# Attention output of a three-stage kernel: the block result turned and normalised by other engines, and carried to token layout by 64-byte transfers

## What is computed

```
xn   = layernorm(x)
attn = gamma * concat_heads(softmax(leaky(q k^T / sqrt(2), 0.2)) v) + xn     # 8 heads, q and k of 2, v of 16 channels
ffn  = mixture of experts on rmsnorm(xn): top 2 of 16, 12 of them MLPs 128-512-128, capacity 1024
out  = x + attn + ffn
```

## Time and profile before

| | us |
|---|---|
| median of three runs | 977.33 |
| profiled execution, its own time | 976.61 |
| span of that execution in the trace | 974.8 |
| VectorE busy | 744.3 (76%) |
| TensorE matmul busy | 883.5 (91%) |
| ScalarE busy | 716.5 (74%) |
| GpSimd busy | 581.7 (60%) |

### The profile page before, as it was taken

One profiled execution on the slowest core, in us unless ns is written; L12 is line 12 of the kernel. 1 busy time (PEld: TensorE's weight loads), 2 busy tenths in 40 slices (PEclk: granted clock), 3 DMA queues, 4 the chain that ended last, 5 costly groups with the idle time before them and its releaser, 6 DMA issues.

```text
span 974.8 us, 19803 instructions
## 1 busy us (share of the span) xinstructions
PE 883.5 (91%) x7619; PEld 365.8 (38%) x7620; DVE 744.3 (76%) x851; ACT 716.5 (74%) x859; POOL 581.7 (60%) x574
## 2 busy tenths in 40 slices
PE   0688249999999999999999989999999999999997
PEld 0444102333333333867767723333333333333332
DVE  6698889999999995001011089999999999999996
ACT  0689878888888887454454468888888888888886
POOL 3355137776676662999999015647566574665770
PEclk9999659999999999999999989999999999999999
DMA  8723100101100011242342210010011002002100
GB/s 228 269 65 72 31 27 30 44 30 36 39 25 28 18 52 58 68 135 92 110 135 78 80 43 26 22 49 20 26 32 39 23 21 64 24 13 62 31 7 22
DMA packets 48163, 55.34 MB, mean 57 GB/s; under 512 B 10714, under 2 KB 35122, under 8 KB 48080
## 3 DMA queue, kind: packets, MB, share of 16 engines
q1 hardware_dynamic: 38464, 44.10, 14.8%
q0 software_dynamic: 8192, 9.37, 3.3%
q10 hardware_dynamic: 1424, 0.76, 0.3%
HBM read 31.58 MB, written 30.02 MB: 63 GB/s over the span
## 4 chain that ended last, share of the span: by engine, by line
PE 77%; ACT 9%; DVE 6%; issue 4%; DMA 1%; SPq 1%; POOLq 0%; ACTq 0%; DVEq 0%
PE ps L765 26%; PE ps L745 15%; PE ps L735 13%; PE ps L825 8%; PE ps L817 8%; ACT pr L636 4%; PE ps L775 3%; ACT ot L628 2%; DVE xn L897 1%; SPq L248 1%; PE ps L695 1%; PE ps L806 1%; ACT y L614 1%; DMA y<-in_x 1%; ACT va L592 1%
## 5 line engine op out<-in xcount | busy, mean ns | idle before, releaser
L1030 DVE TENSOR_SCALAR ps<-ps 128x1024 f32<-128x1024 f32 x512 | 610.7, 1229 | 20.9 <-PE ps L735 6.6
L636 ACT ACTIVATE pr<-ps 128x1024 f32<-128x1024 f32 x512 | 523.3, 1024 | 111.5 <-PE ps L745 101.0
L765 PE MATMUL ps<-pr,vp 128*32 128x256 f32 x4096 | 327.7, 392 | 0.3
L745 PE MATMUL ps<-q,kz 64*128 64x512 bf16 x1024 | 201.7, 391 | 9.2 <-DVE ps L1030 9.1
L735 PE MATMUL ps<-q,kz 62*128 62x512 bf16 x1024 | 199.9, 387 | 7.7 <-DMA q<-parts_dram 1.7
L445 POOL DMA_INDIRECT xs<-eout,idxs x128 | 129.0, 1008 | 108.7 <-ACT pr L636 78.5
L430 POOL DMA_INDIRECT disp<-xn,idx x128 | 125.6, 981 | 47.1 <-issue 35.8
L1042 DVE TENSOR_TENSOR pr<-ps,parts 128x1024 f32<-128x1024 f32 x12 | 14.7, 1225 | 166.1 <-PE ps L825 166.1
L745 PEld LDWEIGHTS ps<-q,kz 64*128 64x128 bf16 x1024 | 49.2, 93 | 222.0 <-DVE ps L1030 117.2
L765 PEld LDWEIGHTS ps<-pr,vp 128*32 128x32 f32 x4096 | 81.2, 108 | 108.1 <-issue 91.3
L663 ACT ACTIVATE pr<-ps,b1s 128x512 f32<-128x512 f32 x96 | 66.0, 687 | 48.8 <-PE ps L817 48.8
(11 more groups left out here) (120 smaller groups left out, 618.6 us busy)
## 6 DMA issues: line engine op xcount, KB each, us to landing
disp<-pr SPq DMA_DIRECT2D x12, 512.0 KB, 4.9
eout<-pr SPq DMA_DIRECT2D x12, 512.0 KB, 2.9
y<-in_x SPq DMA_DIRECT2D x8, 512.0 KB, 8.2
out<-y SPq DMA_DIRECT2D x8, 512.0 KB
w<-in_w1t SPq DMA_DIRECT2D x12, 256.0 KB, 3.1
w<-in_w2t SPq DMA_DIRECT2D x12, 256.0 KB, 3.3
xs<-disp SPq DMA_DIRECT2D x6, 512.0 KB, 4.8
pr<-disp SPq DMA_DIRECT2D x6, 512.0 KB, 4.8
```

The source lines that it names most:

```text
L636: act.activation(pr[:, c % BUFS, 2 * pair:2 * pair + 2, :], ring[i % RING], ACT.Exp, scale=SLOPE).then_inc(S["exps"], 1)
L745: last = pe.matmul(ring[i % RING][:, k, :], kz[r:r + TILE, hg, pair, kc * P:(kc + 1) * P], q2[r:r + TILE, hg, qh * HALF:(qh + 1) * HALF], ...
L765: last = pe.matmul(acc[p % 2][32 * g:32 * g + 32, cols], vp[:, hg, kc, g, :], pr[:, c % BUFS, g % PAIRS * 2 + g // PAIRS, cols], start=(kc ...
L1030: dve.tensor_scalar(s, s, 0.0, 1.0 / SLOPE - 1.0, ALU.max, ALU.mult).then_inc(S["relu"], 1)
```

## The change

ScalarE no longer copies the bank and TensorE no longer transposes it. VectorE turns it in four block transposes of 128 columns (`turn(p, part)`, units 5 to 8), each written to `ot` in SBUF: every 32 x 32 block is transposed by itself. After it, partition 32g + q' of `ot` holds, for head g, the 16 channels and the denominator of queries q', 32 + q', 64 + q', ... (16 of them). VectorE takes the 16 reciprocals (unit 9) from SBUF. The multiply goes to GpSimd (`quotient`). The heads now lie in different groups of partitions, so SP carries the rows to token layout: `spread(p)` issues 16 transfers, one for each head and each 32-query residue, each of 32 partitions x 4 runs of 64 bytes, from `att` to the new tile `moved`. GpSimd adds `moved` to `y` when all 16 have landed, a pass later than before. In SP's program the loads and stores of the attention stretches are laid out pass by pass, and `spread(p - 2)` stands in pass `p`.

```diff
-EVAC = 4
-TURN = 6
-DENOM = 12
-FINISH = 13
+TURN = 5
+PARTS = 4
+BLOCK = 32
@@ SP
+            def spread(p):
+                sp.wait_ge(S["att_rdy"], p + 1)
+                wait_done(sp, "y_att", p - 1)
+                for g in range(HG):
+                    rows = att[BLOCK * g:BLOCK * g + BLOCK, p % 2, :, :].rearrange("q (t r) d -> q t r d", r=P // BLOCK)
+                    for r in range(P // BLOCK):
+                        sp.dma_start(moved[BLOCK * r:BLOCK * r + BLOCK, p % 2, :, g, :], rows[:, :, r, :]
+                                     ).then_inc(S[f"spread{p % 2}"], 16)
...
+            for p in range(BH * NPB):
+                operands_in(p)
+                if p > 1:
+                    spread(p - 2)
...
             sp.wait_ge(S["pv"], BH * NPB * TB)
+            spread(BH * NPB - 2)
             load_expert(1, 1)
+            spread(BH * NPB - 1)
...
+            spread(B * NPB - 2)
+            for s in STORES[B - BH - 1][:-1]:
                 store_sequence(s)
+            spread(B * NPB - 1)
+            store_sequence(B - 1)
@@ GpSimd
+            def quotient(p):
+                pool.wait_ge(S["rg_rdy"], p + 1)
+                wait_done(pool, f"spread{p % 2}", 16 * HG * GT * (p // 2))
+                rows = ot[:, p % 2, :].rearrange("p (q c) -> p q c", c=BLOCK)
+                pool.tensor_tensor(att[:, p % 2, :, :], rows[:, :, 0:DV],
+                                   rg[:, p % 2, :].unsqueeze(2).broadcast_to([P, HALF // BLOCK, DV]), ALU.mult
+                                   ).then_inc(S["att_rdy"], 1)
+
             def add_attention(p):
-                pool.wait_ge(S["att_rdy"], p + 1)
+                pool.wait_ge(S[f"spread{p % 2}"], 16 * HG * GT * (p // 2 + 1))
...
                     move(p)
                     if p > b0 * NPB:
-                        settle(p - 1)
+                        quotient(p - 1)
+                    if p > b0 * NPB + 1:
+                        settle(p - 2)
+                quotient(b1 * NPB - 1)
+                settle(b1 * NPB - 2)
                 settle(b1 * NPB - 1)
@@ ScalarE
-                    if i % UP == EVAC and i > first + UP:
-                        evacuate(i // UP - 1)
...
-                evacuate(end // UP - 1)
@@ TensorE
-                    wait_done(pe, "att_rdy", p - 1)
+                    wait_done(pe, "turned", p - 1)
...
-                    if 0 <= i % UP - TURN < GT and i > first + UP:
-                        turn(i // UP - 1, i % UP - TURN)
...
-                for t in range(GT):
-                    turn(end // UP - 1, t)
...
-                        pe.wait_ge(S["att_rdy"], NPB * BH)
+                        pe.wait_ge(S["turned"], NPB * BH)
@@ VectorE
+            def turn(p, part):
+                if part == 0:
+                    dve.wait_ge(S["pv"], TB * (p + 1))
+                    wait_done(dve, "att_rdy", p - 1)
+                cols = slice(part * HALF // PARTS, (part + 1) * HALF // PARTS)
+                last = dve.transpose(ot[:, p % 2, cols], acc[p % 2][:, cols])
+                if part == PARTS - 1:
+                    last.then_inc(S["turned"], 1)
+
             def denominators(p):
-                dve.wait_ge(S["o_rdy"], p + 1)
-                dve.reciprocal(rg[:], turned(p)[:, :, :, DV]).then_inc(S["rg_rdy"], 1)
+                dve.wait_ge(S["turned"], p + 1)
+                rows = ot[:, p % 2, :].rearrange("p (q c) -> p q c", c=BLOCK)
+                dve.reciprocal(rg[:, p % 2, :], rows[:, :, DV]).then_inc(S["rg_rdy"], 1)
...
+                    if 0 <= i % UP - TURN < PARTS and i > first + UP:
+                        turn(i // UP - 1, i % UP - TURN)
+                    if i % UP == TURN + PARTS and i > first + UP:
+                        denominators(i // UP - 1)
...
+                for part in range(PARTS):
+                    turn(end // UP - 1, part)
                 denominators(end // UP - 1)
-                finish(end // UP - 1)
```

More of the change, by code:

```diff
@@ L151, in build @@
         ot = sb("ot", [P, 2, HALF])
-        rg = sb("rg", [P, GT, HG])
-        att = sb("att", [P, 2, GT, HG, DV])
+        rg = sb("rg", [P, 2, HALF // BLOCK])
+        att = sb("att", [P, 2, HALF // BLOCK, DV])
+        moved = sb("moved", [P, 2, GT, HG, DV])
         rowones = sb("rowones", [1, M], BF16)
@@ L199, in build @@
                  "qz_init weighted gate_rdy row_step route max_rdy off_rdy reset_rdy r_exp cnt_rdy pos_rdy ztile init_rdy kz_init "
-                 "ld0 ld1 vp_rdy s1 relu s2 exps pv acc_evac o_rdy rg_rdy att_rdy y_att "
+                 "ld0 ld1 vp_rdy s1 relu s2 exps pv turned rg_rdy att_rdy spread0 spread1 y_att "
                  "scat staged pool_step carry "
@@ L309, in store_sequence, with operands_in @@
                              y[:, bass.ts(s, TB), :]).then_inc(S["final"], 16)
[L312 to L315, removed]
+            def spread(p):
[6 more added lines that the diff above has]
+                                     ).then_inc(S[f"spread{p % 2}"], 16)
+            def operands_in(p):
+                if p % NPB == 0 and p > 0:
+                    load_operands(p // NPB, 1)
+                if p % NPB == NQ and p // NPB + 1 < B:
+                    load_operands(p // NPB + 1, 0)
+            for hg in range(NHG):
+                load_operands(0, hg)
+            for p in range(BH * NPB):
+                operands_in(p)
+                if p > 1:
+                    spread(p - 2)
             sp.wait_ge(S["scat"], 16 * GS)
@@ L341, in _ @@
                 store_expert(E_MLP - 2 + u)
[L343 to L349, removed]
+            for p in range(BH * NPB, B * NPB):
+                operands_in(p)
+                if p > BH * NPB + 1:
+                    spread(p - 2)
+                if p % NPB == 0 and p > BH * NPB:
+                    for s in STORES[p // NPB - BH - 1]:
+                        store_sequence(s)
+            spread(B * NPB - 2)
+            for s in STORES[B - BH - 1][:-1]:
                 store_sequence(s)
+            spread(B * NPB - 1)
+            store_sequence(B - 1)
             sp.wait_ge(S["final"], 16 * B)
@@ L394, in value_rows @@
                                  va[:, bass.ts(b, TB), hg * HG:(hg + 1) * HG, :]).then_inc(S["vp_rdy"], 1)
+            def quotient(p):
[5 more added lines that the diff above has]
+                                   ).then_inc(S["att_rdy"], 1)
             def add_attention(p):
                 b, hg, qh = p // NPB, p // NQ % NHG, p % NQ
-                pool.wait_ge(S["att_rdy"], p + 1)
+                pool.wait_ge(S[f"spread{p % 2}"], 16 * HG * GT * (p // 2 + 1))
+                pool.sem_inc(S["carry"], 1)
                 ys = y[:, bass.ds(b * TB + qh * GT, GT), hg * HG * DV:(hg + 1) * HG * DV]
-                pool.tensor_tensor(ys, ys, att[:, p % 2, :, :, :].rearrange("p t g d -> p t (g d)"),
+                pool.tensor_tensor(ys, ys, moved[:, p % 2, :, :, :].rearrange("p t g d -> p t (g d)"),
                                    ALU.add).then_inc(S["y_att"], 1)
@@ L471, in gather @@
                     if g > 0 and new:
-                        combine(g - 1, max(p - 1, BH * NPB))
+                        combine(g - 1, max(p - 2, BH * NPB))
                     fetch(g, p, j, len(mine))
                     if g > 0 and not new:
-                        combine(g - 1, max(p - 1, BH * NPB))
+                        combine(g - 1, max(p - 2, BH * NPB))
                     if g == NG - 1:
-                        combine(g, max(p - 1, BH * NPB))
+                        combine(g, max(p - 2, BH * NPB))
             def attention(b0, b1, move):
@@ L492, in settle @@
                 if p >= BH * NPB:
-                    done = share(p + 1, BH * NPB, B * NPB, NG)
+                    done = share(p + 2, BH * NPB, B * NPB, NG)
                     pool.wait_ge(S["comb"], CO0 + (NG if done.stop == NG else max(done.stop - 1, 0)))
@@ L622, in _ @@
             act.wait_ge(S["gate_rdy"], 1)
[L624 to L628, removed]
             def exponentials(i):
@@ L770, in values @@
                     last.then_inc(S["pv"], 1)
[L772 to L777, removed]
             def attention(b0, b1):
@@ L1001, in _ @@
             dve.tensor_tensor(gate, gate, inv.unsqueeze(1).broadcast_to([P, 2, NT]), ALU.mult).then_inc(S["gate_rdy"], 1)
-            def turned(p):
-                return acc[p % 2].rearrange("p (t g c) -> p t g c", g=HG, c=32)
-            def denominators(p):
-                dve.wait_ge(S["o_rdy"], p + 1)
-                dve.reciprocal(rg[:], turned(p)[:, :, :, DV]).then_inc(S["rg_rdy"], 1)
[L1013 to L1018, removed]
+            def turn(p, part):
[6 more added lines that the diff above has]
+                    last.then_inc(S["turned"], 1)
+            def denominators(p):
+                dve.wait_ge(S["turned"], p + 1)
+                rows = ot[:, p % 2, :].rearrange("p (q c) -> p q c", c=BLOCK)
```

(1 more changed line is left out.)

## The result

The changed kernel takes 985.31 us, the median of four runs (985.07 to 986.09), against 977.68 us for the kernel before, measured on the same chip. The ratio is 1.0082, with a 95% interval of 1.0066 to 1.0098: slower by 0.8%. The forecast was 972.3 us, 0.5% faster. Three of all executions, at a granted clock of 0.57 to 0.66, took 1186 to 1352 us; no ratio and no reading of a trace here uses them. The profiled execution took 985.37 us with a span of 983.6, 8.8 us above the span of before.

The account below looks back on a forecast made before the run. A plain unit was held by the ring with TensorE's fixed order, a transpose unit by TensorE, those just after by VectorE. Passes -12.0, end +7.8, boundary -1.2 and +0.4 sum to -5.0 us: 972.3 us, range 966 to 989.

Parts of the forecast that it names:

- The passes: Inside the attention passes, 11 in the first stretch and 19 in the second: about 19.63 us each, -12.0 us.
- Rival 1: VectorE, units 5 to 8: transposes don't overlap and cost 0.28 to 0.38 us each; 977 to 989 us; chance 22%.
- rival 2: Units after the reciprocal: VectorE's catching up stays as short as before, -5.7 in place of -12.0, 978.6 us; chance 10%.
- The end: From the last `values` to the last store: 10.7 us where it was 2.94, so +7.8 us (+7.0 to +10.4).
- rival 3: SP's queue is slower: 0.50 us an issue, landing 2.7, the expert late by 2.4; 976.9 us; chance 10%.
- The boundary: First attention stretch to experts: -1.2 us from TensorE, +0.4 for expert 1's later load (between nothing and +2.4).
- The -1.2: At the start of the experts: TensorE's first transposes of expert 0 follow `values` at once, -1.2 us.
- Covered work: Inside passes: GpSimd's multiplies, SP's 16 issues and the packets are hidden, all costed at nothing.

Follow-up runs that it names:

- experiment 9: Changed kernel without the SBUF transfers (attention rows wrong), with every block transpose done twice, the first into an unread tile: 984.74 us, ratio 1.0075 to the kernel before.
- experiment 6: Changed kernel with each of the 16 transfers a pass made 128 partitions x one 64-byte run, to the same partition: 985.41 us, ratio 1.0069.
- experiment 2: Changed kernel with only load_expert(1, 1) put ahead of spread(10) in SP's program: 983.98 us, ratio 1.0068 to the kernel before.
- experiment 10: Changed kernel with eight of the last pass's 16 transfers issued by ScalarE instead of SP: 979.58 us, ratio 1.0024 to the kernel before.

## Why the prediction was wrong

**The passes: right, and better than forecast.** -12.0 us was the term; the two traces have 0.56 us a pass from 13 to 31 (10.07 over 18) and 6.35 up to pass 11. With 0.55 for pass 11 and the 0.65 in pass 31, that is -17.6. By its steps: a transpose is 0.22 between starts, not 0.24 (-0.08 a pass). The reciprocal, 695.14 - 694.99 = 0.15 and not 0.22, now that it reads SBUF and not the bank (-0.07). After it, L1049 starts 1.11 to 1.13 apart for six units, as forecast. The forecast's 19.63 less these two is 19.48, as measured, and experiment 9 holds it to a doubled transpose. Rival 1 (no overlap) and rival 2 (short catching up) are out.

**The end: the step that failed most.** +7.8 was forecast, measured are +17.9. Two faults. First, its price: "15 intervals of issue at 0.35" came from loads from DRAM, and the upper end from an expert's loads at 0.50. An issue from SBUF to SBUF takes 0.644, outside both ends. The 16 took 10.1 us for 5.25: +4.9. The trace of before had rows of the right kind, `kz<-rowones` at 0.63 (experiment 6), and the prediction did not use them. The last landing and the step to the addition (977.22 to 979.20) were 2.0, near the 2.4 assumed. Second, "with nothing beside it" was wrong: 6.1 us in which SP still issued the transfers of pass 30, because those of pass 29 had waited for GpSimd's quotient, which came 7 us into pass 31. I had read that GpSimd runs into the next pass and used it only for `turn`'s deadline, not for when SP's work then falls. At 0.35 an issue, two batches would have taken 11.2 us from 944.4 and fitted in before 961.0; that is an estimate. The prediction named 0.6 us an issue as the point where the end costs more than the passes give; that is what happened, by 17.9 against 17.6, but only with the 6.1 us of queueing; it stood in no rival, and rival 3 with its 0.50 had the mechanism and too small a price.

**The boundary: right mechanism, same wrong price, and one cost left out.** "Between nothing and +2.4" became 5.74, because 16 issues took 11.1 us instead of 5.3. Another 2.2 us, which the prediction had at nothing, are TensorE's work at a granted clock of 0.50 after the wait. The -1.2 for TensorE's earlier start is in the trace: L825 starts as soon as `values` ends. What the step missed is that spread(11), also 16 issues, stands in front of the next load: experiment 2 shows the wait waiting there.

**Covered work: right.** The DMA share (18% and 21% in two pairs of passes, 14% before) and SP's 10.3 us of issues in a pass of 19.5 cost nothing inside passes: with and without the transfers, passes 13 to 31 take 350.60 us. GpSimd's multiplies stayed in every experiment; that a pass is 19.48 with VectorE's intervals alone leaves nothing for them.

The sum with the measured numbers: passes -17.6, end +17.9, boundary (from pass 11 to 12, without that pass's own 0.55) +6.9, the start of the trace +0.95 and pass 12 +0.67, in all +8.8 for the forecast -5.0. Against the forecast the passes gave 5.6 us more; the end cost 10.1 more and the boundary 7.7 more, and these two steps turned a gain into a loss.

## What to carry to other kernels

A queue's issue time has its own price list: take it from rows with the same kind of source and destination, however small they are in the trace, and count the batches that may still be queued when the last one is ready. Work hidden inside a loop must be priced again at each place where the loop ends, above all when it takes the place of something short. A wait at such a place can also cost by the clock of what runs after it. Here it pays to keep the new way inside the loop and the old way at the ends: 960.5 us, or 958.7 with one transpose of 512 columns, against 978.1 before and 985.3 after.

## What I had not expected of the hardware

- An issue of 8 KB from SBUF to SBUF takes 0.63 to 0.64 us of SP's queue in three shapes, and one of 2 KB in a single run 0.63, while operand loads from DRAM (18 runs of 2 KB, or one) are 0.33 apart. The DMA engines were mostly idle meanwhile: their busy share was 28% while SP issued the last 16. ScalarE's queue, issuing beside SP's, did not slow it (experiment 10), so SP wasn't held back by them. What in an issue inside SBUF takes the longer time stays open.
- A block transpose of 128 x 128 fp32 from PSUM costs VectorE 0.22 us between starts, one of 128 x 512 0.63: the engine starts the next instruction some 0.08 before the shown end, for a transpose as for an ordinary instruction.
- A reciprocal of 16 columns costs 0.15 us between starts when it reads SBUF (0.23 shown), and 0.22 when it reads PSUM (0.25 shown).
- After 5.74 us of waiting, TensorE worked at a granted clock of 0.50, and eight transposes took 1.97 us instead of 1.04; the same followed the wait of 4.86 us in experiment 2. In the traces without such a wait the clock stayed at 1.00 there.
